# A transformer block on one core: a new order of TensorE's work in a step, a larger loop group, three moved operations and new places

## The chip, the cores and the metric

The kernel runs on one core of one Trainium2 chip. A core has TensorE (PE; its weight loads are PEld), VectorE (DVE), ScalarE (ACT), GpSimd (POOL) and SyncE (SP), which issues all the DMAs here. The metric is the device time of one execution in microseconds, the median of several. Everything is in fp32 but a few comparison results.

## The reference

For each of 32 images of 128 channels by 32 x 32 pixels (1024 tokens of 128 values), the reference computes:

```python
x = softmax(Q.T K / sqrt(C)) V + x               # full attention over the 1024 tokens
t = tokens(x)
n = layer_norm(t)
m = mamba(n, forward) + mamba(n reversed, backward)
t = t + m + leaky_relu(layer_norm(m) @ w1.T + b1) @ w2.T + b2
n = layer_norm(t)
w = n @ wr + br                                   # one weight per token
kept = the 511 tokens with the largest w
t = t + n + (w * (gelu(n @ f_w1 + b1) @ f_w2 + b2) where kept, else 0)
```

A mamba direction projects a token to 256 inner values, convolves 4 taps, applies silu, makes dt, B and C, and runs for each of 16 states a recurrence over the 1024 tokens, `h = exp(dt*A) * h + dt*B*u`, with `y = sum over states of C*h`. Then `y + x*D` is multiplied by `silu(z)` and projected back.

## The kernel before

**Tiling.** The mamba of an image is cut in four quarters k: two directions times two chunks of 512 tokens. Each quarter has 16 states, which gives 64 steps n an image. A step holds 256 inner values (two halves of 128 partitions) by 512 tokens for one state.

**A step on each engine.** ACT (`scale_u`, line 860) and POOL (`scale_u`, line 1042) make u*B for two blocks of tokens each, token-wise (`ub`). PE (`turn_ub`, line 518) turns it to channels in PSUM, one half after the other; half 0 waits for both makers, and each half waits until DVE's scan of the step before has read its bank. ACT (`decay`, line 848) makes exp(dt*A) of each half (`da`). DVE runs the recurrence as a scan of each half (`scan`, line 1160). POOL multiplies both halves by C (`times_c`, line 1056, result `g`), which SP has brought from DRAM by a DMA (`load_c`, line 461). PE turns g back and sums it over halves and states in PSUM (`add_y`, line 522), in two parts; part 0 waits for POOL's product, and the end of part 1 frees the buffer of g. ub, da, h and g have two buffers each. The u*B of step n+2 can be made when both halves of step n are turned.

**All the rest is laid between.** A step has four slots, so an image has slots 0 to 255. Tables at the top of the kernel (`AT_...`, `LN_...`) give each other operation its slot: the closing of a finished quarter (`AT_YT`, `AT_SKIP`, `AT_GATE`, `AT_M`), the preparation of the next (`AT_CONV` to `AT_UKEEP`), the attention of the next image (`AT_XT` to `AT_T1`), and the end of the image before (the layer norms, the first MLP, the token weights `AT_W`, their ranking `AT_RANK` and `AT_WK`, the mask `AT_WTIMES`, the second MLP `AT_HID` to `AT_FFN`, and the output). Every engine walks the slots in order, so a slot is a place in its queue, not a time. On PE `aside(SLOTS * n + i)` stands after the pieces of the step. `u_tok`, the token-wise u, is copied from PSUM by DVE at `AT_UKEEP` (line 1248), and the u*B of steps 16, 32, 48 and of the next image's first, made two steps earlier, waits for it. The mask: DVE counts for each token the heavier ones (lines 1275 to 1279), sums, compares with 511 (line 1286), and POOL multiplies the result with the weights (line 1108); DVE uses it in the last sum (line 1293).

**Groups.** `turns(first, count, ...)` emits `count` images in a row without a meeting of the engines. At its end the engines meet, and all semaphores are cleared. The first call has only the first image's attention and first quarter, the second is image 0, and a hardware loop runs groups of `JOINED` images over the next 30; then the last image and its end follow. Before all, one block loads the weights, and ACT and DVE fold some of them once all have landed.

The step on PE, lines 799 to 811:

```python
if n + 1 < ALL or nxt:
    turn_ub(n + 1, 0)
aside(SLOTS * n)
if n + 1 < ALL or nxt:
    turn_ub(n + 1, 1)
aside(SLOTS * n + 1)
if n or last:
    add_y(n - 1, 0)
aside(SLOTS * n + 2)
if n or last:
    add_y(n - 1, 1)
aside(SLOTS * n + 3)
```

Of the kernel before, what the change touches and what calls it, by code (L numbers as in the profile page):

```python
# [5 lines left out]
def conv_attn_mamba_mod_kernel(nc, I, out):  # L6
# [39 lines left out]
    JOINED = 5  # L46
# [4 lines left out]
    AT_YT = (4, 68, 132, 198)  # L51
    AT_SKIP = (8, 74, 137, 202)
    AT_GATE = ((6, 6), (84, 88), (136, 154), (203, 208))
    AT_CONV = ((8, 8, 8, 9), (75, 76, 79, 81), (135, 136, 137, 152), (204, 205, 205, 205))
    AT_PROJ = (17, 74, 140, 203)
    AT_PROJKEEP = (21, 80, 143, 203)
    AT_TAPS = ((25, 26, 27), (84, 87, 87), (148, 156, 158), (208, 209, 209))
    AT_XC = (24, 86, 156, 210)
    AT_Z = ((27, 27), (86, 86), (156, 157), (157, 157))
    AT_ZKEEP = (24, 86, 157, 157)  # L60
    AT_ROWS = ((28, 28), (88, 91), (158, 163), (211, 211))
    AT_ROWKEEP = (28, 95, 164, 213)
    AT_M = ((13, 13), (92, 95), (164, 164), (212, 212))
    AT_MKEEP = (19, 98, 168, 216)
    AT_B = (32, 97, 168, 215)
    AT_BKEEP = (37, 103, 172, 218)
    AT_DT = (35, 101, 170, 215)
    AT_DTCUT = (39, 106, 175, 219)
    AT_DTEXP = (38, 106, 174, 217)
    AT_DTLN = (38, 112, 177, 217)  # L70
    AT_DTMAX = (47, 117, 182, 223)
    AT_U = (51, 118, 183, 226)
    AT_DTKEEP = (51, 116, 180, 231)
    AT_UT = (49, 118, 183, 239)
    AT_UKEEP = (54, 122, 186, 242)
    AT_CSTORE = (22, 114, 171, 212)

    AT_XT = 3
    AT_XTOK = 13
    AT_Q = (11, 12)  # L80
    AT_QKEEP = 12
    AT_K = (19, 20)
    AT_KKEEP = 23
    AT_V = (24, 27)
    AT_VKEEP = 32
    AT_S = (36, 37, 48, 48, 60, 61, 81, 81, 109, 109, 118, 118, 132, 134, 154, 154)
    AT_MAX = (43, 52, 66, 87, 114, 122, 139, 163)
    AT_EXP = (39, 52, 65, 90, 113, 122, 139, 168)
    AT_PT = (43, 52, 67, 96, 114, 124, 144, 173)
    AT_PTKEEP = (42, 55, 67, 97, 115, 123, 145, 174)  # L90
    AT_RINV = (47, 55, 74, 110, 118, 133, 148, 178)
    AT_PV = (46, 47, 55, 56, 68, 70, 106, 107, 116, 116, 127, 131, 148, 148, 178, 179)
    AT_T1 = (50, 61, 83, 110, 120, 133, 153, 182)

    LN_STATS = {0: (131, 194), 1: (15, 30), 2: (211, 213)}
    LN_AGGR = {0: (154, 195), 1: (16, 44), 2: (212, 213)}
    LN_POW = {0: 192, 1: 48, 2: 211}
    LN_APPLY = {0: (197, 197), 1: (58, 67), 2: (216, 216)}
    LN_TURN = {0: 199, 1: 182, 2: 217}
    LN_KEEP = {0: 201, 1: 180, 2: 217}  # L100

    AT_MT = (24, 30)
    AT_B2 = (29, 68)
    AT_T1OLD = 38
    AT_W1 = (184, 185, 189, 189)
    AT_HID1 = (184, 190)
    AT_LEAKY = (191, 195)
    AT_W2 = (195, 195, 195, 195)
    AT_T2 = 199
    AT_BASE = (221, 222)  # L110
    AT_W = (222, 222)
    AT_WKEEP = 221
    AT_WTURN = 225
    AT_WCOL = 229
# [7 lines left out]
    AT_T3 = (243, 247)  # L122
    AT_OUT = 246
    AT_OUTKEEP = 248
    AT_STORE = 244
# [9 lines left out]
    FIRST_T1 = tuple(FIRST + 6 + 4 * i for i in range(8))  # L135

# [5 lines left out]
    with ctx:  # L142
# [127 lines left out]
        zeroed = ctx.enter_context(nc.semaphore("zeroed"))  # L270
        setup_exp = ctx.enter_context(nc.semaphore("setup_exp"))


        with nc.Block() as block:
            loads = [
                (wq[:], I["wq"]), (wk[:], I["wk"]), (wv[:], I["wv"]),
                (bq[:], I["bq"]), (bk[:], I["bk"]),
                (bv_rows[:], I["bv"].to_broadcast([P, C])),
# [20 lines left out]
            @block.sync  # L299
            def _(sp):  # L300
                with nc.allow_non_contiguous_dma(reason="weights, once"):
                    for dst, src in loads:
                        sp.dma_start(dst, src).then_inc(loaded, 16)
                sp.wait_ge(loaded, 16 * len(loads))
# [14 lines left out]
            @block.scalar  # L319
            def _(act):  # L320
                act.wait_ge(loaded, 16 * len(loads))
                act.activation(a_neg[:], a_neg[:], ACT.Exp).then_inc(setup_exp, 1)

            @block.vector
            def _(dve):
                dve.wait_ge(loaded, 16 * len(loads))

                dve.tensor_scalar(bq[:], bq[:], SCALE, None, ALU.mult)
                dve.tensor_scalar(b1_low[:], b1[:], SLOPE, None, ALU.mult)
                dve.tensor_copy(wr_cols[:], wr[:].to_broadcast([C, P]))  # L330

                for r in range(DIRS):
                    for tap in range(KCONV):
                        dve.tensor_tensor(w_conv[:, r, tap, :], w_conv[:, r, tap, :], in_cols[:, r, 0:P], ALU.mult)
                dve.wait_ge(setup_exp, 1)
                dve.tensor_scalar(a_neg[:], a_neg[:], -1.0, None, ALU.mult)
# [65 lines left out]
            (w_col_kept, 1), (w_kept_made, 1), (w_made, 1), (w_row_kept, 1), (w_turned, 1), (x_loaded, 16),  # L402
# [9 lines left out]
        def turns(first, count, last, now, nxt):  # L412
# [32 lines left out]
            with nc.Block() as block:  # L445

                def sp_turn(sp, j):
# [31 lines left out]
                    if nxt:  # L479
                        sp.dma_start(x_in[:], I["x"][image + 1]).then_inc(x_loaded, 16)  # L480
# [25 lines left out]
                def pe_turn(pe, j):  # L506
# [103 lines left out]
                    def prepare(at, k):  # L610
# [3 lines left out]
                        if at == AT_PROJ[k]:  # L614
                            if k == QUARTERS - 1:
# [6 lines left out]
                        for tap in due(AT_CONV[k], at):  # L622
                            if tap == 0 and k == QUARTERS - 1:
# [104 lines left out]
                    def attend_next(at):  # L728
                        if at == AT_XT:
                            pe.wait_ge(x_loaded, since(x_loaded, 16))  # L730
# [93 lines left out]
                def act_turn(act, j):  # L824
# [52 lines left out]
                    def prepare(at, k):  # L877
# [133 lines left out]
                    if not now:  # L1011
                        for at in range(SLOTS * ALL):
                            aside(at)
                        if nxt:
                            for n in range(LEAD):
# [9 lines left out]
                def pool_turn(pool, j):  # L1025
# [50 lines left out]
                    def aside(at):  # L1076
# [8 lines left out]
                        if last:  # L1085
# [52 lines left out]
                def dve_turn(dve, j):  # L1138
# [71 lines left out]
                    def prepare(at, k):  # L1210
# [35 lines left out]
                        if at == AT_UKEEP[k]:  # L1246
                            dve.wait_ge(u_turned, since(u_turned, prep(k, 1, 1)))
                            dve.tensor_copy(u_tok[:, side, :, :].rearrange("p b d -> p (b d)"), banks(Y)  # L1248
                                            ).then_inc(u_kept, 1)

                    def finish_last(at):
# [29 lines left out]
                        if at == AT_WK:  # L1281
# [4 lines left out]
                            dve.tensor_scalar(is_kept[:], rank[:], float(KEPT), None, ALU.is_lt).then_inc(ranked, 1)  # L1286
                        for part in due(AT_T3, at):
                            if part == 0:
                                dve.wait_ge(w_kept_made, since(w_kept_made, 1))
# [50 lines left out]
                    if not now:  # L1340
                        for at in range(SLOTS * ALL):
                            aside(at)
# [70 lines left out]
```

## Time and profile before

| what | us |
|---|---|
| median of 3 runs | 8347.58 (8346.27 to 8347.81) |
| the profiled execution | 8358.25 |
| its span | 8356.5 |
| from the span's start to the first scan | 135.0 |
| image 0, scan to scan | 240.8 |
| an image inside a group | 252.8 |
| the 32nd image's first scan to the end | 356.8 |

The page gives for each engine its busy time over the span; a view by stretches gives the same for any piece of it, with the clock granted to PE (1.00 is full speed), which shows which engine is full where. The view in order of time gives start and length of groups of instructions. Matmul rows are modelled to their ends and overlap, so the distance of their starts says more of PE's cost than their length. Places in the image are named by the first scan of its steps: image 18 begins at 4697.6, and its pieces of 8 steps begin at 4697.6, 4729.8, 4758.6, 4788.3, 4817.6, 4845.6, 4877.1 and 4911.6.

### The profile page before, as it was taken

What the parts mean: (1) busy time and instruction counts of PE and PEld (TensorE: products, weight loads), DVE (VectorE), ACT (ScalarE), POOL (GpSimd) and SP (SyncE); (2) the same over time, 40 slices, a digit from 0 to 9 for tenths busy, and PEclk for the clock granted to TensorE, in tenths of its full rate; (3) what the DMA queues carried; (4) which work ended last, traced back from release to release, by engine and by line L of the source; (5) the groups of instructions that cost most, each with busy time, mean ns of one, the idle gap of its engine ahead of it and who ended that gap; (6) DMA issues with size and microseconds to landing.
All of it is one profiled execution on the core that took longest, in us unless ns stands there. A gap on an engine that the chain in (4) does not pass through costs nothing. (4 is left out here: it accounts for less than half of the span.)

```text
span 8356.5 us, 152516 instructions
## 1 busy us (share of the span) xinstructions
PE 7891.8 (94%) x53760; PEld 6159.6 (74%) x53760; DVE 7365.4 (88%) x10156; ACT 6933.8 (83%) x11874; POOL 7487.6 (90%) x7051
## 2 busy tenths in 40 slices
PE   6999999999999999999999999999999999999986
PEld 4777777777777777777777777777777777777765
DVE  4899899898999898999989999989999989999985
ACT  4888888888888888888888888888888888888874
POOL 3999999899999899999999999989999999999985
PEclk9999999999999999999999999999999999999998
DMA  1222222222222222222222222222222222222221
GB/s 49 75 68 79 75 76 73 71 72 77 75 74 74 72 73 76 74 74 69 73 78 75 74 75 72 73 75 74 74 75 72 74 75 74 74 71 72 78 71 35
DMA packets 321339, 604.11 MB, mean 72 GB/s; under 512 B 40961, under 2 KB 43714, under 8 KB 320578
## 3 DMA queue, kind: packets, MB, share of 16 engines
q1 hardware_dynamic: 320578, 594.31, 23.0%
q8 instruction: 435, 7.13, 0.4%
q14 instruction: 326, 2.67, 0.1%
HBM read 556.42 MB, written 20.97 MB: 69 GB/s over the span
## 5 line engine op out<-in xcount | busy, mean ns | idle before, releaser
L1056 POOL TENSOR_TENSOR g<-h,c_all 128x1024 f32<-128x1024 f32 x2048 | 4861.9, 2374 | 210.4 <-DVE h L1160 119.6
L848 ACT ACTIVATE da<-dt,a_neg 128x512 f32<-128x512 f32 x4096 | 2771.4, 715 | 165.4 <-DVE h L1160 158.4
L1160 DVE TENSOR_TENSOR_SCAN h<-da,ps 128x512 f32<-128x512 f32 x2048 | 2432.2, 1210 | 447.2 <-ACT da L848 215.1
L1160 DVE TENSOR_TENSOR_SCAN h<-da,h,ps 128x512 f32<-128x512 f32 x2048 | 2544.8, 1270 | 214.7 <-PE ps L518 80.4
L518 PE MATMUL ps<-ident,ub 128*128 128x128 f32 x16384 | 2373.2, 276 | 126.0 <-DVE h L1160 107.0
L518 PEld LDWEIGHTS ps<-ident,ub 128*128 128x128 f32 x16384 | 1886.0, 141 | 761.7 <-issue 466.4
L522 PE MATMUL ps<-ident,g 128*128 128x128 f32 x16384 | 2248.7, 275 | 12.8 <-POOL g L1056 9.4
L522 PEld LDWEIGHTS ps<-ident,g 128*128 128x128 f32 x16384 | 1892.0, 141 | 421.3 <-issue 391.1
L1042 POOL TENSOR_SCALAR ub<-u_tok,b_tok 128x256 f32<-128x256 f32 x4096 | 1932.8, 488 | 208.9 <-DVE u_tok L1248 190.4
L860 ACT ACTIVATE ub<-u_tok,b_tok 128x256 f32<-128x256 f32 x4096 | 1845.8, 500 | 310.0 <-PE ps L518 219.5
L515 PE MATMUL ps<-v_tok,probs_t 128*128 128x128 f32 x4096 | 543.3, 278 | 16.4 <-ACT probs_t L966 16.4
L515 PEld LDWEIGHTS ps<-v_tok,probs_t 128*128 128x128 f32 x4096 | 491.5, 192 | 34.5 <-ACT probs_t L966 30.4
L515 PE MATMUL ps<-k_all,q 128*128 128x512 f32 x1024 | 502.1, 598 | 7.5 <-DVE t L1315 3.1
L515 PE MATMUL ps<-x_pad,w_conv 128*128 128x512 f32 x1024 | 504.9, 595 | 0.2 <-DVE xc L1193 0.2
L837 ACT ACT_TABLE_LOAD x352 | 451.6, 1283 | 6.2
L972 ACT ACTIVATE probs<-ps,nmax 128x1024 f32<-128x1024 f32 x256 | 284.5, 1111 | 106.8 <-DVE nmax L1303 100.8
L1303 DVE TENSOR_REDUCE nmax<-ps 128x1 f32<-128x1024 f32 x256 | 308.7, 1206 | 40.5 <-PE ps L515 40.5
L966 ACT ACTIVATE probs_t<-ps 128x1024 f32<-128x1024 f32 x256 | 262.2, 1024 | 86.5 <-PE ps L518 84.3
L1083 POOL TENSOR_TENSOR xc<-xc,sz 128x512 f32<-128x512 f32 x256 | 326.4, 1281 | 6.2 <-DVE xc L1193 6.2
L518 PE MATMUL ps<-ident,probs 128*128 128x128 f32 x2048 | 270.7, 275 | 59.5 <-ACT probs L972 59.5
L515 PE MATMUL ps<-tile_b,f_w 128*128 128x512 f32 x512 | 261.0, 633 | 63.4 <-ACT hid L945 40.1
L1218 DVE SCALAR_TENSOR_TENSOR ps<-x_proj,w_taps,ps 128x512 f32<-128x512 f32 x384 | 283.8, 739 | 25.8 <-ACT ps L890 12.4
(125 smaller groups left out, 9152.8 us busy)
## 6 DMA issues: line engine op xcount, KB each, us to landing
c_all<-c_rows SPq DMA_DIRECT2D x2048, 256.0 KB, 3.1
x_in<-in_x SPq DMA_DIRECT2D x32, 512.0 KB, 5.6
t_old<-t SPq DMA_DIRECT2D x32, 512.0 KB, 4.4
out<-tile_b SPq DMA_DIRECT2D x32, 512.0 KB, 2.8
c_rows<-rows SPq DMA_DIRECT2D x128, 32.0 KB, 2.7
w_conv<-in_conv_rows SPq DMA_DIRECT2D x1, 512.0 KB
f_w<-in_f_w SPq DMA_DIRECT2D x2, 256.0 KB
hid<-in_in_proj SPq DMA_DIRECT2D x1, 256.0 KB
```

The costliest lines, as they stand in the source:

```text
L515: return nc.tensor.matmul(o, a, b, start=first, stop=last)
L518: return nc.tensor.transpose(o, src, ident[:])
L522: return nc.tensor.matmul(o, src, ident[:], start=first, stop=last, is_transpose=True)
L837: nc.scalar.preload_act_table_set(name)
L848: act.activation(da[:, n % 2, half, :], dt[:, slot, half, :], ACT.Exp, scale=a_neg[:, r, half, s:s + 1]).then_inc(da_made, 1)
L860: t = act.activation(ub[:, n % 2, b, :], u_tok[:, slot, b, :], ACT.Copy, scale=b_tok[:, slot, b, s:s + 1])
L972: act.activation(probs[:], banks(att(i)), ACT.Exp, bias=nmax[:, i:i + 1], accum_out=rowsum[:, i:i + 1]).then_inc(probs_made, 1)
L1042: t = pool.tensor_scalar(ub[:, n % 2, b, :], u_tok[:, slot, b, :], b_tok[:, slot, b, s:s + 1], 1.0, ALU.mult, ALU.mult)
L1056: pool.tensor_tensor(g[:, n % 2, :, :], h[:, n % 2, :, at:at + BANK], c_all[:, n % RING, :].unsqueeze(1).to_broadcast([P, NH, BANK]), ALU.mult
L1083: pool.tensor_tensor(xc[:, slot, half, :], xc[:, slot, half, :], sz[:, slot % NCH, half, :], ALU.mult).then_inc(y_gated, 1)
L1160: dve.tensor_tensor_scan(h[:, n % 2, half, at:at + BANK], da[:, n % 2, half, :], ps[:, DB + half, :], before, ALU.mult, ALU.add).then_inc( ...
L1303: dve.tensor_reduce(nmax[:, i:i + 1], banks(att(i)), AX.X, ALU.max, negate=True).then_inc(max_made, 1)
```

## The change

Five things change.

- On PE, the sum's part 1 (`add_y(n - 1, 0)`) moves between the halves of u*B: a step is now half 0, sum part 1, half 1, sum part 2, with a slot after each.
- `JOINED` is 15 for 5.
- The first block waits on DVE for seven loads alone (x of image 0, now first, and the attention's weights); x of image 0 is no longer loaded in the first turn. The folding of the other weights moves to the first turn, at slot 60 on ACT and DVE, and PE's first quarter and ACT's first u*B wait for it (`weights_made`).
- The copy of u_tok goes from DVE to ACT; the mask's product goes from POOL to DVE, as eight products of one column.
- Nearly all places are new.

```diff
-    JOINED = 5
+    JOINED = 15
...
-    AT_CONV = ((8, 8, 8, 9), (75, 76, 79, 81), (135, 136, 137, 152), (204, 205, 205, 205))
+    AT_CONV = ((7, 7, 7, 8), (78, 81, 81, 83), (140, 141, 142, 152), (209, 210, 210, 210))
-    AT_GATE = ((6, 6), (84, 88), (136, 154), (203, 208))
+    AT_GATE = ((7, 7), (80, 87), (160, 160), (209, 213))
-    AT_Z = ((27, 27), (86, 86), (156, 157), (157, 157))
+    AT_Z = ((24, 25), (85, 85), (160, 160), (160, 161))
-    AT_DTCUT = (39, 106, 175, 219)
+    AT_DTCUT = (42, 103, 174, 225)
-    AT_DTMAX = (47, 117, 182, 223)
+    AT_DTMAX = (47, 112, 178, 230)
-    AT_UT = (49, 118, 183, 239)
+    AT_UT = (53, 117, 180, 236)
-    AT_UKEEP = (54, 122, 186, 242)
+    AT_UKEEP = (54, 116, 180, 236)
-    AT_B2 = (29, 68)
+    AT_B2 = (27, 97)
-    AT_BASE = (221, 222)
+    AT_BASE = (225, 227)
-    AT_EARLIER = 223
+    AT_EARLIER = 229
-    AT_RANK = (230, 231, 231, 232, 234, 234, 234, 239)
+    AT_RANK = (235, 235, 237, 238, 238, 238, 239, 240)
-    AT_WK = 240
-    AT_WTIMES = 237
+    AT_WK = 243
-    AT_HID = (226, 226, 229, 229, 231, 231, 232, 232)
-    AT_GELU = (227, 227, 228, 228)
-    AT_FFN = (233, 233, 233, 234, 239, 239, 240, 242)
+    AT_HID = (230, 230, 232, 232, 235, 235, 236, 236)
+    AT_GELU = (231, 233, 233, 233)
+    AT_FFN = (239, 239, 239, 239, 241, 241, 242, 242)
...
+            first_loads = [
+                (x_in[:], I["x"][0]), (bq[:], I["bq"]), (wq[:], I["wq"]), (bv_rows[:], I["bv"].to_broadcast([P, C])),
+                (wk[:], I["wk"]), (bk[:], I["bk"]), (wv[:], I["wv"]),
+            ]
...
+                dve.wait_ge(first_loaded, 16 * len(first_loads))
...
                         aside(SLOTS * n)
+                        if n or last:
+                            add_y(n - 1, 0)
+                        aside(SLOTS * n + 1)
                         if n + 1 < ALL or nxt:
                             turn_ub(n + 1, 1)
-                        aside(SLOTS * n + 1)
-                        if n or last:
-                            add_y(n - 1, 0)
                         aside(SLOTS * n + 2)
...
+                        if at == AT_UKEEP[k]:
+                            act.wait_ge(u_turned, since(u_turned, prep(k, 1, 1)))
+                            act.activation(u_tok[:, side, :, :].rearrange("p b d -> p (b d)"), banks(Y), ACT.Copy
+                                           ).then_inc(u_kept, 1)
...
+                            if nxt and at == SETUP:
+                                act.wait_ge(loaded, all_loaded)
+                                tables("natural_log_exp_and_others")
+                                act.activation(a_neg[:], a_neg[:], ACT.Exp).then_inc(setup_exp, 1)
...
-                            if at == AT_WTIMES:
-                                pool.wait_ge(ranked, since(ranked, 1))
-                                pool.tensor_tensor(w_kept[:], is_kept[:], w_col[:], ALU.mult).then_inc(w_kept_made, 1)
...
+                            dve.wait_ge(ranked, since(ranked, 1))
+                            for i in range(NB):
+                                dve.tensor_scalar(w_kept[:, i:i + 1], is_kept[:, i:i + 1], w_col[:, i:i + 1], None, ALU.mult
+                                                  ).then_inc(w_kept_made, 1)
```

## Rows read from the trace of the kernel before

**Rows 1.** Busy time of each engine over the span, with instructions, from the page.

```profile
PE 7891.8 (94%) x53760; PEld 6159.6 (74%) x53760; DVE 7365.4 (88%) x10156; ACT 6933.8 (83%) x11874; POOL 7487.6 (90%) x7051
```

**Rows 2.** Busy time, clock and DMA by stretch: image 18, three of eight pieces.

```profile
4697.60:4729.80 32.20, 31.43 (x202) 23.30 (x200) 26.37 (x36) 24.48 (x41) 32.20 (x31) 1.00 0.24 81
4877.10:4911.60 34.50, 33.95 (x231) 26.34 (x232) 32.70 (x55) 32.55 (x61) 33.83 (x37) 1.00 0.20 63
4911.60:4950.40 38.80, 35.40 (x234) 26.80 (x233) 36.97 (x75) 28.79 (x46) 28.94 (x27) 1.00 0.22 64
```

**Rows 3.** In order of time, image 18, steps 15 to 17 (start us, length us).

```profile
4757.62 1.02 PE L515 MATMUL ps<-k_all,q 128*128 128x512 f32 x2
...
4758.48 0.60 PE L518 MATMUL ps<-ident,ub 128*128 128x128 f32 x4
...
4758.92 1.02 PE L515 MATMUL ps<-k_all,q 128*128 128x512 f32 x2
...
4759.24 2.37 POOL L1056 TENSOR_TENSOR g<-h,c_all 128x1024 f32<-128x1024 f32 x1
...
4760.65 1.09 PE L518 MATMUL ps<-ident,ub 128*128 128x128 f32 x8
...
4764.37 2.44 DVE L1160 TENSOR_TENSOR_SCAN h<-da,h,ps 128x512 f32<-128x512 f32 x2
```

**Rows 4.** The same view, behind a boundary of the loop's groups.

```profile
1648.63 0.90 PE L518 MATMUL ps<-ident,ub 128*128 128x128 f32 x3 [4.17 <-DVE h L1160]
```

**Rows 5.** By stretch: last and first image at a boundary, then a plain one.

```profile
1390.50:1647.40 256.90, 245.37 (x1692) 192.04 (x1689) 229.92 (x318) 217.12 (x373) 234.80 (x223) 1.00 0.24 74
1647.40:1902.20 254.80, 245.82 (x1670) 193.87 (x1671) 230.00 (x317) 215.87 (x371) 232.92 (x219) 0.98 0.23 73
4697.60:4950.40 252.80, 244.30 (x1682) 191.09 (x1681) 229.91 (x317) 216.36 (x372) 233.90 (x221) 1.00 0.24 74
```

**Rows 6.** By stretch: the first 5.35 us behind that boundary.

```profile
1647.35:1652.70 5.35, 4.07 (x18) 3.68 (x19) 3.65 (x4) 4.88 (x8) 5.35 (x4) 0.50 0.66 204
```

**Rows 7.** In order of time: the start of the kernel.

```profile
17.78 1.96 SPq L303 DMA_DIRECT2D w_rows<-in_x_proj  x3
...
21.65 0.15 DVE L328 TENSOR_SCALAR bq<-bq 128x1 f32<-128x1 f32 x1 [21.65 <-DMA w_rows<-in_x_proj]
...
27.61 1.97 PE L518 MATMUL ps<-ident,x_in 128*128 128x128 f32 x8 [27.61 <-DMA x_in<-in_x]
```

**Rows 8.** Who waited for whom: us in total, times, longest us.

```profile
POOL w_kept L1108 <- DVE is_kept L1286: 249.0, 32, 13.4
...
PEld ps L518 <- DVE h L1160: 208.2, 401, 4.6
POOL ub L1042 <- DVE u_tok L1248: 190.4, 64, 28.5
```

**Rows 9.** Groups of instructions by line: busy us, mean ns | idle before, releasers.

```profile
L1056 POOL TENSOR_TENSOR g<-h,c_all 128x1024 f32<-128x1024 f32 x2048 | 4861.9, 2374 | 210.4 <-DVE h L1160 119.6 <-PE ps L522 67.4 <-issue 17.9
...
L1042 POOL TENSOR_SCALAR ub<-u_tok,b_tok 128x256 f32<-128x256 f32 x4096 | 1932.8, 488 | 208.9 <-DVE u_tok L1248 190.4 <-PE ps L518 15.1 <-POOLq L1350 3.5
...
L1277 DVE TENSOR_SCALAR_CACHE_REDUCE compared<-w_row,w_col 128x1024 bf16<-128x1024 f32 (+7 forms) x256 | 207.4, 810 | 0.5 <-POOL tile_a L1103 0.5
...
L1238 DVE SCALAR_TENSOR_TENSOR ps<-ps,b_dt,dt 128x512 f32<-128x512 f32 x256 | 179.2, 746 | 3.9 <-ACT dt L915 2.2
...
L1275 DVE TENSOR_SCALAR_CACHE_REDUCE compared<-w_row,w_col 128x128 bf16<-128x128 f32 (+6 forms) x224 | 164.7, 735 | 0.0
...
L1248 DVE COPY u_tok<-ps 128x1024 f32<-128x1024 f32 x128 | 154.5, 1207 | 3.8 <-PE ps L518 3.7
...
L919 ACT ACTIVATE dt<-ps 128x1024 f32<-128x1024 f32 x128 | 130.3, 1018 | 58.7 <-DVE u L1245 58.7
...
L1279 DVE TENSOR_SCALAR_CACHE_REDUCE tied<-tile_a,w_col 128x128 bf16<-128x128 f32 x256 | 88.1, 344 | 0.0
...
L1279 DVE DVE_READ_ACCUMULATOR tied<-tile_a,w_col 128x1 f32 x256 | 21.8, 85 | 0.0
```

More of the change, by code:

```diff
@@ L74, in conv_attn_mamba_mod_kernel @@
-    AT_UT = (49, 118, 183, 239)
-    AT_UKEEP = (54, 122, 186, 242)
-    AT_CSTORE = (22, 114, 171, 212)
-    AT_XT = 3
[L79 to L102, printed above, removed]
@@ L122, in conv_attn_mamba_mod_kernel @@
[L122 to L125, printed above, removed]
+    AT_YT = (4, 68, 132, 197)
+    AT_SKIP = (7, 74, 140, 202)
+    AT_GATE = ((7, 7), (80, 87), (160, 160), (209, 213))
+    AT_CONV = ((7, 7, 7, 8), (78, 81, 81, 83), (140, 141, 142, 152), (209, 210, 210, 210))
+    AT_PROJ = (14, 74, 144, 209)
+    AT_PROJKEEP = (18, 81, 150, 210)
+    AT_TAPS = ((20, 24, 24), (82, 82, 86), (154, 160, 161), (212, 215, 215))
+    AT_XC = (23, 83, 159, 214)
+    AT_Z = ((24, 25), (85, 85), (160, 160), (160, 161))
@@ new lines, in conv_attn_mamba_mod_kernel @@
+    AT_ZKEEP = (24, 85, 159, 160)
+    AT_ROWS = ((28, 31), (88, 89), (162, 165), (215, 216))
+    AT_ROWKEEP = (33, 88, 165, 217)
+    AT_M = ((10, 10), (90, 91), (166, 166), (217, 217))
+    AT_MKEEP = (15, 97, 171, 220)
+    AT_B = (36, 97, 169, 220)
+    AT_BKEEP = (40, 100, 173, 223)
+    AT_DT = (39, 99, 170, 220)
+    AT_DTCUT = (42, 103, 174, 225)
+    AT_DTEXP = (41, 101, 174, 223)
+    AT_DTLN = (41, 101, 174, 225)
+    AT_DTMAX = (47, 112, 178, 230)
+    AT_U = (50, 114, 179, 230)
+    AT_DTKEEP = (52, 114, 177, 232)
@@ new lines, in conv_attn_mamba_mod_kernel @@
+    AT_UT = (53, 117, 180, 236)
+    AT_UKEEP = (54, 116, 180, 236)
+    AT_CSTORE = (43, 90, 157, 205)
+    AT_XT = 3
+    AT_XTOK = 8
+    AT_Q = (16, 18)
+    AT_QKEEP = 20
+    AT_K = (21, 23)
+    AT_KKEEP = 24
+    AT_V = (28, 28)
+    AT_VKEEP = 29
+    AT_S = (33, 34, 44, 44, 62, 62, 77, 83, 106, 106, 120, 122, 136, 138, 158, 158)
+    AT_MAX = (39, 48, 66, 87, 111, 126, 142, 164)
+    AT_EXP = (37, 49, 66, 90, 110, 124, 142, 172)
+    AT_PT = (39, 50, 67, 92, 110, 127, 148, 175)
+    AT_PTKEEP = (39, 53, 69, 99, 111, 127, 150, 174)
@@ new lines, in conv_attn_mamba_mod_kernel @@
+    AT_RINV = (44, 55, 74, 101, 120, 130, 158, 183)
+    AT_PV = (42, 42, 55, 58, 71, 73, 100, 103, 113, 115, 131, 131, 154, 155, 176, 178)
+    AT_T1 = (46, 63, 77, 107, 121, 137, 158, 184)
+    LN_STATS = {0: (130, 190), 1: (12, 17), 2: (208, 210)}
+    LN_AGGR = {0: (160, 190), 1: (14, 42), 2: (208, 214)}
+    LN_POW = {0: 197, 1: 44, 2: 215}
+    LN_APPLY = {0: (198, 201), 1: (62, 77), 2: (218, 218)}
+    LN_TURN = {0: 206, 1: 184, 2: 224}
+    LN_KEEP = {0: 207, 1: 184, 2: 224}
+    AT_MT = (18, 40)
@@ new lines, in conv_attn_mamba_mod_kernel @@
+    AT_B2 = (27, 97)
+    AT_T1OLD = 28
+    AT_W1 = (188, 190, 195, 195)
+    AT_HID1 = (190, 194)
+    AT_LEAKY = (195, 199)
+    AT_W2 = (199, 199, 199, 203)
+    AT_T2 = 207
+    AT_BASE = (225, 227)
+    AT_W = (227, 227)
+    AT_WKEEP = 226
+    AT_WTURN = 230
+    AT_WCOL = 233
+    AT_EARLIER = 229
[4 more added lines that the diff above has]
+    AT_FFN = (239, 239, 239, 239, 241, 241, 242, 242)
@@ L128, in conv_attn_mamba_mod_kernel @@
+    AT_T3 = (245, 246)
+    AT_OUT = 247
+    AT_OUTKEEP = 249
+    AT_STORE = 240
     FIRST = SLOTS * 12
@@ L135, in conv_attn_mamba_mod_kernel @@
     FIRST_T1 = tuple(FIRST + 6 + 4 * i for i in range(8))
+    SETUP = FIRST + 12
     def due(slots, g):
@@ L270, in conv_attn_mamba_mod_kernel @@
         zeroed = ctx.enter_context(nc.semaphore("zeroed"))
+        first_loaded = ctx.enter_context(nc.semaphore("first_loaded"))
         setup_exp = ctx.enter_context(nc.semaphore("setup_exp"))
+        weights_made = ctx.enter_context(nc.semaphore("weights_made"))
         with nc.Block() as block:
+            first_loads = [
+                (x_in[:], I["x"][0]), (bq[:], I["bq"]), (wq[:], I["wq"]), (bv_rows[:], I["bv"].to_broadcast([P, C])),
+                (wk[:], I["wk"]), (bk[:], I["bk"]), (wv[:], I["wv"]),
+            ]
             loads = [
-                (wq[:], I["wq"]), (wk[:], I["wk"]), (wv[:], I["wv"]),
-                (bq[:], I["bq"]), (bk[:], I["bk"]),
-                (bv_rows[:], I["bv"].to_broadcast([P, C])),
                 (in_cols, I["in_proj"][:, :, 0:DI].rearrange("r c e -> c r e")),
@@ L301, in _ @@
                 with nc.allow_non_contiguous_dma(reason="weights, once"):
+                    for dst, src in first_loads:
+                        sp.dma_start(dst, src).then_inc(first_loaded, 16)
                     for dst, src in loads:
                         sp.dma_start(dst, src).then_inc(loaded, 16)
-                sp.wait_ge(loaded, 16 * len(loads))
             @block.gpsimd
@@ L316, in _ @@
                                    base=0, pattern=[[-1, P]], channel_multiplier=1)
[L319 to L322, printed above, removed]
             @block.vector
             def _(dve):
-                dve.wait_ge(loaded, 16 * len(loads))
+                dve.wait_ge(first_loaded, 16 * len(first_loads))
                 dve.tensor_scalar(bq[:], bq[:], SCALE, None, ALU.mult)
[L329 to L336, printed above, removed]
+        all_loaded = 16 * len(loads)
         x_loaded, stored = sem("x_loaded"), sem("stored")
@@ L401, in conv_attn_mamba_mod_kernel @@
             (u_made, 4), (u_turned, 4), (ub_made, 64), (ub_made_pool, 64), (v_kept, 1), (v_made, 1),
-            (w_col_kept, 1), (w_kept_made, 1), (w_made, 1), (w_row_kept, 1), (w_turned, 1), (x_loaded, 16),
+            (w_col_kept, 1), (w_kept_made, 8), (w_made, 1), (w_row_kept, 1), (w_turned, 1), (x_loaded, 16),
             (xc_kept, 8), (xc_made, 4), (xt_kept, 1), (xt_made, 1), (y_gated, 8), (y_kept, 4), (y_made, 64),
@@ L478, in sp_turn @@
                         sp.wait_ge(v_made, since(v_made, 0))
-                    if nxt:
+                    if nxt and now:
                         sp.dma_start(x_in[:], I["x"][image + 1]).then_inc(x_loaded, 16)
@@ L614, in prepare @@
                         if at == AT_PROJ[k]:
+                            if not now:
+                                pe.wait_ge(weights_made, 1)
                             if k == QUARTERS - 1:
@@ L622, in prepare @@
                         for tap in due(AT_CONV[k], at):
+                            if tap == 0 and not now:
+                                pe.wait_ge(weights_made, 1)
                             if tap == 0 and k == QUARTERS - 1:
@@ L729, in attend_next @@
                         if at == AT_XT:
-                            pe.wait_ge(x_loaded, since(x_loaded, 16))
+                            if now:
+                                pe.wait_ge(x_loaded, since(x_loaded, 16))
                             if joined:
@@ L1012, in act_turn @@
                         for at in range(SLOTS * ALL):
+                            if nxt and at == SETUP:
+                                act.wait_ge(loaded, all_loaded)
+                                tables("natural_log_exp_and_others")
+                                act.activation(a_neg[:], a_neg[:], ACT.Exp).then_inc(setup_exp, 1)
                             aside(at)
                         if nxt:
+                            act.wait_ge(weights_made, 1)
                             for n in range(LEAD):
@@ L1245, in prepare @@
                             dve.tensor_tensor(u[:], ps[:, Y:Y + NH, :], xc[:, slot, :, :], ALU.mult).then_inc(u_made, 1)
[L1246 to L1249, printed above, removed]
                     def finish_last(at):
@@ L1286, in finish_last @@
                             dve.tensor_scalar(is_kept[:], rank[:], float(KEPT), None, ALU.is_lt).then_inc(ranked, 1)
+                            dve.wait_ge(ranked, since(ranked, 1))
+                            for i in range(NB):
+                                dve.tensor_scalar(w_kept[:, i:i + 1], is_kept[:, i:i + 1], w_col[:, i:i + 1], None, ALU.mult
+                                                  ).then_inc(w_kept_made, 1)
                         for part in due(AT_T3, at):
                             if part == 0:
-                                dve.wait_ge(w_kept_made, since(w_kept_made, 1))
+                                dve.wait_ge(w_kept_made, since(w_kept_made, NB))
                             dve.wait_ge(base_made, since(base_made, part + 1))
@@ L1341, in dve_turn @@
                         for at in range(SLOTS * ALL):
+                            if nxt and at == SETUP:
+                                dve.wait_ge(loaded, all_loaded)
+                                dve.tensor_scalar(b1_low[:], b1[:], SLOPE, None, ALU.mult)
+                                dve.tensor_copy(wr_cols[:], wr[:].to_broadcast([C, P]))
+                                for r in range(DIRS):
+                                    for tap in range(KCONV):
+                                        dve.tensor_tensor(w_conv[:, r, tap, :], w_conv[:, r, tap, :], in_cols[:, r, 0:P],
+                                                          ALU.mult)
+                                dve.wait_ge(setup_exp, 1)
+                                dve.tensor_scalar(a_neg[:], a_neg[:], -1.0, None, ALU.mult).then_inc(weights_made, 1)
                             aside(at)
```

28 lines of the change are left out of this document (removed).

## The prediction

> **What bounds the kernel now.** I read the page's busy shares first. PE is busy 94% of the span, POOL 90%, DVE 88%, ACT 83% [rows 1]: no engine has room by itself, so the question is which one is full in which stretch. An image inside a group of the loop takes 252.8 us, from its first scan to the next image's first scan. The view by stretches cuts one such image in pieces of 8 steps. In the first piece POOL is busy 32.20 of 32.20 us, in the seventh 33.83 of 34.50, and in the eighth DVE 36.97 of 38.80 while POOL works 28.94 [rows 2]. So POOL sets the pace early, POOL and PE together in the middle, DVE at the end. In the first and the seventh piece PE too is 98% busy by the view, but a matmul's row there carries its latency: the two of 512 columns at 4757.62 show 1.02 us and the flips behind them start 0.86 later; four flips of u*B show 0.60 and what follows starts 0.44 later [rows 3].
>
> Were the view's PE row a floor (244.3 of 252.8, the sum of all eight pieces), nothing could win over 8.5 us an image. The Trainium skill, "Perfetto Trace Analysis", section Identifying the Most-Contended Engine, says that matmul busy time is no measure of PE's headroom and that the share of weight loading is. Weight loading is 74% here [rows 1], so by that rule the ceiling is the busier of POOL and DVE. My forecast stays below both ceilings.
>
> **Part 1, the loop's group.** JOINED goes from 5 to 15, so 30 images take 2 groups for 6 and four boundaries go. At one, PE stands 4.17 us for the first scan behind it [rows 4]. The image that ends at it takes 256.9 us and the one after it 254.8, beside 252.8 for a plain one [rows 5]: 4.1 + 2.0. The second loss need not recur in full, so I take 5.2 us (bounds 4.1 and 6.1): 4 x 5.2 = 21 us (16 to 24). Part of the 2.0 is the clock: over the 5.35 us after the stop, PE's granted clock is 0.50, the 1.2 GHz level [rows 6]; it is 1.00 in the pieces of a plain image [rows 2].
>
> **Part 2, the start.** The first block now waits for nothing but issues the same 33 loads and one for x. Those end at 17.78 + 1.96 = 19.7 us [rows 7], plus some 0.45 for x; DVE waits for seven of them. If the block still ends in a meeting of all engines, PE's first flip moves from 27.61 to about 20.5: 7.1 us less. The weight set-up on DVE and ACT, 2.1 us from 21.65 [rows 7] on by its eleven short operations, moves into the first attention. That chain is serial, and DVE waits in it, so between none and all of the 2.1 returns. I take 6 us (5 to 7). If engines could leave the block alone, x, issued first, would set the start and up to 19 us would go; I don't count on it.
>
> **Part 3, work that changes engine, per image.** Four copies of u_tok leave DVE (1.207 us each by mean, -4.8) and come to ACT, whose nearest row, the copy of dt from the same PSUM banks, takes 1.018 us: +4.1 on ACT. w_kept leaves POOL: its wait for is_kept was 249.0 us in 32, 7.8 an image [rows 8], and DVE gets eight one-column products and a wait. Nearest rows: one-column reads at 85 ns [rows 9] and the 344 ns of the 128-column comparison; by the 85 they are 0.7 us, and I take 1.1 with the wait, bounds 0.7 and 2.8. DVE's balance is -3.7. POOL's 7.8 us of waiting is in the eighth piece, where DVE is full, so its loss is cover: it is worth nothing by itself, and what is late next is the ranking on DVE. POOL's waits for u_tok are 190.4 us; less the 28.5 of the start they are 5.2 an image [rows 8]. The copies moved from slots 122, 186, 242 to 116, 180, 236, ahead of the u*B that needs them at 120, 184, 248, so most of that wait goes; what follows on POOL there is the same products, and DVE is as full in those steps. ACT's own queue behind each copy is the decay of two steps later.
>
> **Part 4, the places.** I laid every instruction of both tables into its step, with its row's time (POOL: 2.374 for g, 2 x 0.47 for u*B, and for a half sum or a gate, with half of g's columns, 1.28; DVE: 1.2 a scan, 1.4 for a pair of 746 ns operations, 16.5 for the ranking, from 207.4 + 164.7 + 88.1 over 32 and 23 or 24 reads of 85 ns; PE: 0.44 for four flips, 0.86 for 512 columns, and for four products a tenth more than that) [rows 3, 9], scaled each engine to its busy time of the image, and took the largest engine in each 8 steps. Before: 32.3 POOL, 28.3 POOL, 29.8 POOL, 27.8 DVE, 30.6 PE, 27.0 PE, 36.8 POOL, 39.0 DVE = 251.7 us; the trace has 252.8, and 32.2, 34.5 and 38.8 in the pieces shown [rows 2]. After: 31.0, 29.6, 29.9, 27.3, 27.3, 29.4, 33.2, 41.6 = 249.2 us. The first loses half of the bias sum (slot 68 to 97). The fifth hands four gate products (3.4 us of PE) to the sixth. The seventh loses three POOL operations (two half sums and the mask of earlier weights) to the eighth, where POOL has room. The eighth gains on DVE, the bound there: the cut and the maximum of dt go from slots 219 and 223 to 225 and 230, +2.8, less the u_tok copy, plus the products. The same count in stretches of 4 steps gives -1.3 and of 16 steps -1.8. I take -2.0 us an image (-0.5 to -3.5).
>
> **Part 5, PE's order.** Sum part 1 now stands between the halves of u*B. Two edges. For it: PE waits for DVE's scan 208.2 us in 401 times [rows 8], of which seven boundaries are some 30; going through image 18 in order of time, 4 of its 5 us are ahead of half 1, and a sum can fill them. Against it: the sum needs POOL's product, and half 1 comes 0.44 us later, with what the slot holds. In one step of the image the product ends at 4761.61 and half 1 started at about 4761.09: the sum would wait 0.5 us; but the scan's pair that eats this half started its first part at 4764.37 and so had over 2 us [rows 3]. In 13 of its 64 steps the product is late by the new order, 5.7 us in all, mostly in such slack. SP, ACT and POOL keep their order. I take 0, with -4 and +4.5 us an image as bounds.
>
> **Sum.** 30 full images and the last: 31 x 2.0 = 62; 62 + 21 + 6 = 89. The profiled execution took 8358.25 us with a span of 8356.5, so it would come to 8269; the median of the runs is 10.7 below it, 8347.58, and gives 8259, say 8260 us.
>
> **Rivals.** (a) Only the loop and the start pay, and the places balance better on paper than on queues with waits: 8348 - 27 = 8321. For it: DVE, bound at the end, gets longer there. 18%. (b) The sums fill PE's waits as well, 4 us an image more: 8259 - 124 = 8135. For it: the 4 us; against it, POOL and DVE are full while PE waits. 12%. (c) Slower than before: sum part 1 holds half 1. Price: 13 late products and a later half 1 in the 19 steps of this image where its scan followed within 0.5 us (19 x 0.44 = 8.4); half of the 14.1 together, less the half of PE's own 5 us of waits that goes, is 4.5 us an image, and 2.5 after the 2.0 of the places. Then 8348 - 27 + 31 x 2.5 = 8398. It decides from 2.9 us an image (89 / 31) onward. Against it: where POOL is full, its u*B is what PE would wait for next anyway. 12%. (d) The clock. The ranks stood at slots 230 to 239 and now at 235 to 240, four of them (8.3 us) between two scans, where PE has 5.6 us of work (four flips, four of the sum, half the second MLP's output with 0.9 for its bias) before it needs the next scan. PE would stand for 8.3 + 1.2 - 5.6 = 3.9 us, as at a boundary, and a clock of 0.50 for 5.35 us [rows 6] costs 2.7 us of PE an image: 8259 + 31 x 2.7 = 8343. 8%, since PE, 35.40 of 38.80 us busy in this piece [rows 2], may come late to that place. The Trainium skill, "TensorE: Matmul & The Clock Gate", section Part 1: The HAM clock gate, says the same of idling: the lower level is the default and activity lifts it; the trace agrees at the boundary.
>
> **How the numbers follow.** Forecast 8260 at 50%; its own range, by the bounds of parts 1 to 4, is 8205 to 8310. The range for 8 in 10 is 8160 to 8345: it takes in (a) and (d), leaves out (c) and most of (b). About 0.2% (17 us) is what a measurement of this kernel tells from no change. Faster by more: 50 + 18 + 12 = 80%; within: (d), 8%; slower: 12%.
>
> **What would show it.** Right: one boundary inside the loop and a plain image of about 250.8 us; PE's first flip near 20.5 us; POOL with no wait for is_kept and hardly one for u_tok; the last 8 steps longer by 1 to 3 us, the seventh piece shorter. Wrong: PE waiting for POOL's product over 3 us an image, DVE's scans waiting for PE more than before, or a granted clock below 1.00 near step 60.

## The result

| | us, median of the runs compared |
|---|---|
| before | 8346.37 |
| after | 8371.96 |
| ratio | 1.0031, 95% interval 1.0023 to 1.004 |
| predicted | 8260 (8160 to 8345) |

The kernel is 25.6 us slower, where 89 us less were forecast. The profiled execution of after has a span of 8379.3 us. Against [rows 1], its page has 100 us more on ACT and 33 less on DVE, and PE and POOL are as busy as before.

```profile
PE 7892.6 (94%) x53760; PEld 6152.6 (73%) x53760; DVE 7332.3 (88%) x10284; ACT 7034.2 (84%) x12002; POOL 7481.8 (89%) x7019
```

The view by stretches, in its columns as in [rows 2]: first the whole of image 20 of after, then its third, sixth, seventh and eighth pieces of 8 steps (the third begins at step 16), and the image that ends at the one boundary left in the loop.

```profile
5216.70:5470.90 254.20, 244.34 (x1681) 191.03 (x1682) 228.86 (x321) 219.58 (x376) 233.61 (x220) 1.00 0.24 74
...
5277.60:5309.50 31.90, 31.53 (x205) 23.71 (x206) 26.86 (x27) 28.53 (x54) 30.54 (x29) 1.00 0.25 74
5363.30:5395.50 32.20, 31.29 (x216) 24.06 (x215) 27.41 (x41) 28.94 (x48) 28.45 (x26) 1.00 0.23 67
5395.50:5428.70 33.20, 32.06 (x215) 24.38 (x214) 30.11 (x45) 30.63 (x57) 32.54 (x34) 1.00 0.20 62
5428.70:5470.90 42.20, 38.52 (x252) 28.59 (x250) 41.22 (x86) 32.49 (x50) 29.53 (x28) 1.00 0.17 55
...
3935.40:4194.60 259.20, 245.87 (x1692) 192.42 (x1692) 228.91 (x322) 220.31 (x377) 234.56 (x222) 1.00 0.24 74
```

An image grew where [rows 5] has 252.8: this one takes 254.2, and 254.7 is the median of images 2 to 30, boundaries included. The last 8 steps take 42.2 us for 38.8 and DVE is busy in 41.22 of them [rows 2]. The seventh piece fell by 1.3 us to the 33.2 forecast, where the count had let it fall by 3.6, from 36.8; the third, forecast at 29.9, takes 31.9, and the sixth, forecast at 29.4, takes 32.2.

The view in order of time around the mask shows what fills DVE's last piece.

```profile
5458.08 2.35 POOL L1064 TENSOR_TENSOR g<-h,c_all 128x1024 f32<-128x1024 f32 x1 [5.45 <-DVE h L1165]
5458.11 2.37 DVE L1287 TENSOR_SCALAR is_kept<-rank 128x8 f32<-128x8 f32 x1
...
5460.51 1.06 DVE L1290 TENSOR_SCALAR w_kept<-is_kept,w_col 128x1 f32<-128x1 f32 x8
```

Eight numbers a partition take 2.37 us, from 0.03 us behind the start of POOL's product to 0.05 behind its end. All 32 executions of this comparison, in the view of its tile, in before and in after:

```profile
L1286 DVE TENSOR_SCALAR is_kept<-rank x32: 171/172/174, 617.1 to 8335.7; 128x8 f32<-128x8 f32 x32
...
L1287 DVE TENSOR_SCALAR is_kept<-rank x32: 172/2362/2369, 611.8 to 8355.8; 128x8 f32<-128x8 f32 x32
```

The columns are least, median and most in ns. In after 31 of the 32 last 2355 or more, and each of them starts 0.02 to 0.03 us behind a product of POOL; the one of the last image, with nothing on POOL beside it, lasts 172 as all did before. It never shows as a wait, since the profile counts it as busy.

Last, who waited for whom in after. DVE's scans wait 341.7 us for PE where they waited 181 in before, and PE waits 281.5 us (its weight loads) for POOL's product, 8.8 an image.

```profile
POOL g L1064 <- DVE h L1165: 403.0, 339, 5.5
DVE h L1165 <- PE ps L512: 341.7, 559, 2.3
PEld ps L516 <- POOL g L1064: 281.5, 490, 4.1
ACT ub L859 <- PE ps L512: 277.4, 330, 4.1
...
POOL ub L1050 <- ACT u_tok L921: 30.7, 2, 29.8
```

### The profile page after: what moved, and what is told of

It is laid out like the page before. It is cut to its first block and busy times, and to the rows that moved or that the text cites. A ratio compares the mean times of both kernels' runs of the same rounds, so it can differ in the third digit from the quotient of the medians.

```text
span 8379.3 us, 152633 instructions
## 1 busy us (share of the span) xinstructions
PE 7892.6 (94%) x53760; PEld 6152.6 (73%) x53760; DVE 7332.3 (88%) x10284; ACT 7034.2 (84%) x12002; POOL 7481.8 (89%) x7019
## 5 line engine op out<-in xcount | busy, mean ns | idle before, releaser
L516 PE MATMUL ps<-ident,g 128*128 128x128 f32 x16384 | 2496.5, 275 | 148.4 <-POOL g L1064 144.4
L512 PE MATMUL ps<-ident,ub 128*128 128x128 f32 x16384 | 2489.1, 275 | 77.3 <-DVE h L1165 64.1
L516 PEld LDWEIGHTS ps<-ident,g 128*128 128x128 f32 x16384 | 1919.3, 141 | 809.2 <-issue 519.7
L512 PEld LDWEIGHTS ps<-ident,ub 128*128 128x128 f32 x16384 | 1915.6, 141 | 510.6 <-issue 409.3
L1050 POOL TENSOR_SCALAR ub<-u_tok,b_tok 128x256 f32<-128x256 f32 x4096 | 1912.0, 480 | 180.2 <-PE ps L512 144.2
L509 PE MATMUL ps<-v_tok,probs_t 128*128 128x128 f32 x4096 | 539.4, 278 | 36.8 <-ACT probs_t L969 36.8
```

Of the source, the lines that this page charges most:

```text
L509: return nc.tensor.matmul(o, a, b, start=first, stop=last)
L512: return nc.tensor.transpose(o, src, ident[:])
L516: return nc.tensor.matmul(o, src, ident[:], start=first, stop=last, is_transpose=True)
L1050: t = pool.tensor_scalar(ub[:, n % 2, b, :], u_tok[:, slot, b, :], b_tok[:, slot, b, s:s + 1], 1.0, ALU.mult, ALU.mult)
```

## The experiments

Times are medians; the change against before is taken against the runs of before on the same chip (8347.92, 8350.27, 8348.48 and 8353.36 us in the four groups below). Where two runs are compared, each is first taken against its own before. The interval of a ratio is some 0.1% to either side, 8 to 13 us. The diffs show the main lines, without all conditions and increments of semaphores; `...` stands for lines left out.

### First group: the mask, the order, the loop

**a_mask_fused**, on the kernel after:

```diff
-dve.tensor_scalar(is_kept[:], rank[:], float(KEPT), None, ALU.is_lt).then_inc(ranked, 1)
-dve.wait_ge(ranked, since(ranked, 1))
 for i in range(NB):
-    dve.tensor_scalar(w_kept[:, i:i + 1], is_kept[:, i:i + 1], w_col[:, i:i + 1], None, ALU.mult)
+    dve.tensor_scalar(w_kept[:, i:i + 1], rank[:, i:i + 1], float(KEPT), w_col[:, i:i + 1], ALU.is_lt, ALU.mult)
```

> The kernel after, with is_kept left out: the eight one-column products of the mask compare the rank and multiply by the weight in one instruction each. In the trace of after, is_kept lasts 2.36 us (0.17 before) and ends with POOL's product of g. Theory M (the mask): DVE's comparison of SBUF to SBUF cannot run beside POOL's product and costs DVE, which is full there, 2.2 us an image; without it 31 x 2.2 = 68 us go: 8372 - 68 = 8304. Theory O (the order of PE) and theory P (the places): DVE's time there is covered by others, under 15 us go: 8357 to 8372.

Measured: 8336.48 us, ratio to before 0.9986 (0.9977 to 0.9995). Against after, each on its own before, 37 us are gone. That is half of the 68: the comparison blocked DVE for 31 x 2.2 us, and half of what was freed doesn't show in the time: the median of images 2 to 30 falls by 1.1 us, from 254.7 to 253.6. The last piece of image 20 shows 40.70 us for 42.20, with DVE no longer full:

```profile
5407.00:5447.70 40.70, 37.82 (x252) 28.69 (x250) 39.11 (x86) 31.85 (x49) 29.63 (x28) 1.00 0.17 55
```

**a_order_old**, on the kernel after (and **b_order_new** its reverse, on the kernel before):

```diff
+turn_ub(n + 1, 1)
+aside(SLOTS * n + 1)
 add_y(n - 1, 0)
-aside(SLOTS * n + 1)
-turn_ub(n + 1, 1)
```

> The kernel after with PE's old order in a step (both halves of u*B, then both sum parts); all else as in after. Theory O: the sum's wait for POOL (426 us in the rows of after against 36 before) and the later half 1 (DVE's scans wait 342 us for PE against 181) cost 1 to 2 us an image; the old order gives 30 to 60 us back: 8312 to 8342. Theory M and theory P: the order is a wash or the new places need it, 8360 to 8400.

Measured: 8471.63 us, 1.0148 (1.0132 to 1.0164). The new places need the new order: 98 us more than after, and above both ranges.

> The kernel before with the new order of PE alone, its own places kept. Theory O: slower by 1 to 3 us an image, 8380 to 8440. The prediction's bounds were -4 to +4.5 us an image. Theory M: within 20 us of before, 8326 to 8366.

Measured: 8903.83 us, 1.0664 (1.0649 to 1.0679), 556 us more, 18 an image, four times the bound that the prediction gave the order and far above both ranges. Its waits:

```profile
DVE h L1160 <- PE ps L518: 711.4, 919, 4.0
ACT ub L860 <- PE ps L518: 699.0, 623, 3.8
...
POOL ub L1042 <- PE ps L518: 402.2, 353, 6.9
```

In before these are 181, 219 and 15 us.

**b_joined**, on the kernel before, `JOINED = 15`.

> The kernel before with groups of 15 images for 5. The prediction: four boundaries at 5.2 us go, 21 us (16 to 24): 8325. Rival, since images inside the groups of after vary less but one of them (17) took 258.0 us: what a boundary costs comes back elsewhere, 8340 to 8350.

Measured: 8323.11 us, 0.9970 (0.9958 to 0.9981). 24.8 us for four boundaries, 6.2 each, near the whole 4.1 + 2.0 of [rows 5] (16 to 35 us in all, by the interval). It didn't come back elsewhere, as the rival had it.

### Second group: the ring of u*B, and the outer part alone

**b_order_new_ub4** and **a_fused_ub4**, with `UBS = 4`:

```diff
-ub = sb("ub", [P, 2, QB, DI])
+ub = sb("ub", [P, UBS, QB, DI])
... # PE, ACT and POOL take buffer n % UBS for n % 2
-if now and (n > LEAD or joined):
-    act.wait_ge(dbx_made, since(dbx_made, NH * (n - 2)))
+if now and (n > UBS or joined):
+    act.wait_ge(dbx_made, since(dbx_made, NH * (n - UBS)))
```

> The kernel before with the new order of PE, and four buffers for u*B in place of two; the makers of u*B still run two steps ahead. In the new order alone (8904 us) ACT waits 699 us and POOL 402 us for PE before u*B, beside 219 and 15. Theory R (the ring): half 1 is turned later, that frees the buffer of u*B later, and ACT and POOL, which make the next u*B in their queues' order, stop with all that stands behind it. With four buffers that wait is gone, and most of the 557 us: 8340 to 8500. Theory H (half 1): the scans of half 1 get their data later, whatever the buffers: 8750 to 8900.

Measured: 8743.98 us, 1.0469 (1.0453 to 1.0485). 162 of the 556 us go, 394 stay: between the two ranges, 6 us below the second. Both theories hold a part.

> The kernel after with the mask of one instruction a column (8336 us) and four buffers for u*B. There ACT waits 320 and POOL 144 us for PE before u*B. Theory R: part of these 464 us is on the path even with the new places, 1 to 3 us an image: 8245 to 8305. Theory P (the places were made for two buffers, and the stops are covered by others): 8320 to 8340.

Measured: 8336.71 us, 0.9987 (0.9978 to 0.9997), the same as with two buffers. With the places made for the order, the ring isn't on the path.

**b_outer**: the kernel before with `JOINED = 15`, the seven first loads, and the folding in the first turn; order, places, u_tok and the mask as in before.

> The kernel before with groups of 15 images and the start of after (first loads, folding in the first turn); order, places, u_tok's copy and the mask as before. Groups alone gave 8323; the first scan comes at 131.8 us in after for 135.0. So 8323 - 3 = 8320 by that, 8317 by the 6 us of the prediction.

Measured: 8316.40 us, 0.9962 (0.9949 to 0.9976). **b_outer_fused** puts the mask on it in a_mask_fused's form, at slot 240, and takes POOL's wait away:

> The same with the mask on DVE, one instruction a column (eight, some 0.12 us each). POOL's wait for the comparison, 7.8 us an image, goes, and DVE, full there, gets 1 us an image. The prediction's reading (the wait is cover, DVE is the bound): 8320 + 31 x 1 = 8351. Rival: POOL's stop holds the products and then the scans (DVE waits for POOL's g 101 us in before), so that up to 2 us an image come back: 8290 to 8325.

Measured: 8320.40 us, 0.9966 (0.9952 to 0.9980), not to be told from b_outer. The 31 us that the prediction's reading gave DVE's products don't appear. Either POOL's 7.8 us of waiting an image were cover and the products cost little, or a small gain and a small cost cancel; this run can't tell the two apart. The blocked comparison isn't in it.

### Third group: which part of the order costs, and where u_tok is copied

**b_sum_only** and **b_slot_only**, on the kernel before:

```diff
 turn_ub(n + 1, 0)
 aside(SLOTS * n)
+add_y(n - 1, 0)            # b_sum_only
+aside(SLOTS * n + 1)       # b_slot_only
 turn_ub(n + 1, 1)
-aside(SLOTS * n + 1)       # b_slot_only
-add_y(n - 1, 0)            # b_sum_only
```

> The kernel before with sum part 1 between the halves of u*B, and the work of slot 1 behind half 1, as before: half 1 comes 0.44 us later and waits for POOL's product, and nothing else comes between. The full new order cost 557 us. Theory S (the slot's work): the 29 us of an image's PE work that stand in slots 1 now hold half 1, and the scans of half 1; the sum alone costs under 150: 8350 to 8500. Theory W (the sum and its wait for the product): 8650 to 8900.

Measured: 8460.57 us, 1.0131 (1.0116 to 1.0147), 112 us more.

> The kernel before with the work of slot 1 ahead of half 1 and the sum where it was. Theory S: most of the 557 us: 8600 to 8850. Theory W: under 8500.

Measured: 8734.29 us, 1.0464 (1.0448 to 1.0480), 386 us more. 112 + 386 = 498 of 556: two thirds of the order's price on old places are the work of slot 1 that now precedes half 1, a fifth is the sum with its wait, and the rest is what they do together. In b_sum_only the scans' waits for PE are 316 us in 615 times; the sum is cheap, but not free.

**b_outer_uact**: b_outer with `AT_UKEEP = (54, 119, 183, 242)`, the copy on ACT as in after. **a_fused_udve**: a_mask_fused with the copy back on DVE, at the slots of after.

> The kernel before with groups of 15 and the new start (8316 us) and u_tok's copy on ACT, at slots 54, 119, 183 and 242 (119 and 183 for 122 and 186, since ACT needs its own copy at 120 and 184). The prediction: DVE loses 4.8 us an image and POOL's 5.2 us of waiting for u_tok go. Where DVE is full at these places, 1 to 2 us an image: 8254 to 8285. Rival: the copy needs the flips of u at slots 118 and 183, so ACT stops for PE and with it the decays behind: 8300 to 8340.

Measured: 8354.60 us, 1.0009 (1.0000 to 1.0018), 40 us more than b_outer, and above both ranges.

> The kernel after with the mask of one instruction a column (8336 us) and u_tok's copy back on DVE, same slots. If the move to ACT was worth the 4.8 us of DVE where DVE is full: 31 x 1 to 2 = 8367 to 8398. If the move brought nothing: 8325 to 8345.

Measured: 8742.20 us, 1.0472 (1.0458 to 1.0486), 405 us more than a_mask_fused, and far above both ranges. Either move costs time: neither table bears the other's engine. The waits say in part why. The first row is b_outer_uact, where POOL's wait for u_tok stays at the 190 us and more of before, since the slots hardly moved (and DVE's scans wait 260.8 us for PE, for 177.0 in b_outer):

```profile
POOL ub L1051 <- ACT u_tok L922: 211.9, 65, 29.8
```

and this one is a_fused_udve, where DVE reaches the copy before PE has made the flips, and stops with its scans behind it:

```profile
DVE u_tok L1249 <- PE ps L512: 312.9, 128, 4.5
```

### Fourth group: the new places, the form of the comparison, the ring in the old order

**a_fused_slot_behind**: a_mask_fused with `add_y(n - 1, 0)`, `turn_ub(n + 1, 1)`, then `aside(SLOTS * n + 1)` and `aside(SLOTS * n + 2)`.

> The kernel after with the mask of one instruction a column (8336 us), and the work of slot 1 behind half 1 in place of ahead of it, as in b_sum_only. On the places of before, the slot's work ahead of half 1 cost 386 us and the sum 112. If it costs in the kernel after too (DVE's scans wait there 343 us for PE), the time falls below the 8316 us of the old order and old places: 8230 to 8310. If the new places keep light steps' work in slot 1 and count on it, the swap brings nothing or costs: 8330 to 8420.

Measured: 8417.18 us, 1.0075 (1.0062 to 1.0088), 75 us more than a_mask_fused, each on its own before. Giving half 1 its data earlier costs time with these places.

**a_mask_cols**: after, with is_kept in eight comparisons of one column.

> The kernel after, with is_kept made as eight comparisons of one column in place of one of eight columns; the eight products stay. Theory of the blocked comparison: it is the form with eight columns that can't run beside POOL's product, so eight short ones, seven instructions more and 0.7 us more of DVE an image, still come out near the kernel with no is_kept at all (8336): 8335 to 8355. If DVE's stop were one for the count or the wait on its own result, not for the form, it stays or grows: 8370 to 8395.

Measured: 8342.06 us, 0.9986 (0.9977 to 0.9995), the ratio of a_mask_fused. The same place in image 20, in order of time: eight comparisons in 0.58 us, beside POOL's product of 2.36.

```profile
5434.17 2.36 POOL L1064 TENSOR_TENSOR g<-h,c_all 128x1024 f32<-128x1024 f32 x1 [5.45 <-DVE h L1165]
...
5434.19 0.58 DVE L1288 TENSOR_SCALAR is_kept<-rank 128x1 f32<-128x1 f32 x8
...
5434.80 1.06 DVE L1292 TENSOR_SCALAR w_kept<-is_kept,w_col 128x1 f32<-128x1 f32 x8
```

It is the form that was blocked, not the count of instructions. The Trainium skill, "SBUF — State Buffer", section Who interferes with whom, says that DVE and GpSimd share a second pair of SBUF ports, that a `tensor_scalar` can run in a mode which takes it, and that the second to issue stands until the first is done. Both traces agree with the blocking: 2.36 us with eight columns; with one column, 0.14 us each and no stop. In which mode an instruction ran, no trace here shows.

**b_outer_ub4**: b_outer with four buffers of u*B.

> The kernel before with groups of 15, the new start (8316 us) and four buffers for u*B. In before ACT waits 219 us for PE ahead of u*B, 6.5 an image. In the new order alone four buffers gave 160 us back, in the kernel after none. If part of the 219 is on the path of the old order: 8270 to 8305. If ACT's stops are covered: 8310 to 8322.

Measured: 8315.08 us, 0.9953 (0.9941 to 0.9966), b_outer again, within the intervals. The two are the fastest versions of the study, 34 to 38 us under before, with the order and the places of before.

## Why the prediction was wrong

By differences to before, the result closes. The loop and the start give 33.9 us (b_outer), the order, the places, u_tok's copy and the mask's move together cost 22.4 (from there to a_mask_fused, at -11.4), and the blocked comparison costs 37.0 (from there to after, at +25.6). The forecast had -27, -62 and nothing for the three. So the miss, 114 us, is made of 84 by the places and the order (parts 3 to 5) and 37 by the comparison, less the 7 that the outer part gave beyond its forecast.

**Part 1, right, a little low.** 24.8 us for 21, just above the upper bound of 24 and within the noise of it.

**Part 2, right in its mechanism.** The first block still ends in a meeting; PE's first flip comes at 21.25 us for 20.5 forecast and 27.61 before.

```profile
18.60 1.96 SPq L310 DMA_DIRECT2D w_rows<-in_x_proj  x3
...
21.25 1.94 PE L512 MATMUL ps<-ident,x_in 128*128 128x128 f32 x8 [21.25 <-PEq L277]
```

The first scan moved by 3.2 us in after and 5.3 in b_outer (129.7 for 135.0); in a_mask_fused, with the start of after, it moved by 5.8, so one execution gives it only within some us. b_outer is 7 to 9 us under b_joined's gain alone, for 6.

**Part 3, wrong in one price, and that turned a small gain into a loss.** "Nearest rows: one-column reads at 85 ns" priced the eight products, and rightly: 1.06 us as they stand. The comparison ahead of them got no price of its own; it had taken 0.17 us in before. Those executions had a quiet POOL: it stood waiting for that very instruction, 249.0 us in all [rows 8]. The step that failed is "its loss is cover: it is worth nothing by itself". For time b_outer_fused has nothing against it, but the wait also kept POOL off while DVE compared. In after, POOL's product starts with the end of the same scan that lets DVE go on, so the two meet in 31 of 32 images. The cost, 2.2 us an image in DVE's full piece, appears on the path with about half its size. POOL's waits for u_tok went as forecast, to 0.9 us beside the start's 29.8.

**Part 4, the step with the wrong sign, and the largest part of the miss.** "I took the largest engine in each 8 steps" gave 249.2 us an image, 2.5 less than its 251.7 for before. Without the blocked comparison the median of images 2 to 30 is 253.6 us, and 252.7 in b_outer: 0.9 more.

The count's gain stood mainly in the seventh piece (3.6 us) and the fifth (3.3). Just there it had laid too much on before: 36.8 and 30.6, where the trace has 34.5 and 28.0. Most of the gain was this excess; from b_outer to a_mask_fused the two pieces of image 20 give 1.2 and 1.4 us. The sixth was short in both, 27.0 for 31.5 before and 29.4 for 32.2 after. The third, with a change of 0.1 by the count, grew by 2.0 us: PE has more matmuls there and is busy nearly throughout. First b_outer, then a_mask_fused:

```profile
5238.00:5267.70 29.70, 29.03 (x188) 21.54 (x187) 26.44 (x26) 25.33 (x45) 29.70 (x28) 1.00 0.23 72
...
5255.90:5287.70 31.80, 31.43 (x205) 23.61 (x205) 26.82 (x26) 28.37 (x54) 30.46 (x29) 1.00 0.25 74
```

That the sum fitted before within 1.1 us was luck, misses of both signs, and I took the fit as a proof. Such a count knows how much work stands in 8 steps, not whether each piece is there when its reader comes, and it isn't even a floor for a piece, as the seventh and the fifth of before show. It gives the same 249.2 us for after and for after in the old order, which lie 98 us apart, and for a_mask_fused and a_fused_slot_behind, 75 apart. For a_fused_udve's 405 us it has at most the 4.8 us an image of the copies, 149.

**Part 5, the order, mis-sized by four on the places it was worked out from.** "Half 1 comes 0.44 us later, with what the slot holds" names the cause, and the sum then priced 0.44 us alone. The slot's work was the larger part (386 us of 556 on old places). And "SP, ACT and POOL keep their order. I take 0" left out who waits for half 1 beside the scan: both makers of u*B, for their buffer, with decays, exponentials and products queued behind (162 us by four buffers). The fill of PE's waits did occur, but at another's cost: in after PE's weight loads wait 65 us for DVE's scan, for 208, and 281 for POOL's product. On the new places nothing shows the order to be bad by itself; taking it back costs 98 us. Each table is made for its order and its engine, and swapping the order, a part of it or the copy's engine alone costs 40 to 556 us. What of the 22 us comes from the order, from the places and from u_tok's copy isn't settled: no run has good places for another mixture.

**Rivals.** (c), slower by the order, had the right sign and the signs in the waits, but its mechanism isn't shown as the cause: the old order on these places is slower still. The waits named as signs don't decide it either, since a_mask_fused, which is faster than before, has them too (343.4 us of the scans for PE, 300.3 of PE's weight loads for POOL). (d), the clock: PE didn't stand at the ranks. The granted clock of the last piece is 1.00; the second MLP's products fill the time between the two scans. (a) was right for the loop and the start (34 us for 27), but the places and the order, at nothing by it, cost 22, and it has no blocked comparison.

## What to carry to other kernels

Price an instruction that changes its neighbours by whom it will run beside, not by its old duration: a wait that costs nothing can be what keeps two instructions apart. A count of work per stretch can't rank two schedules that differ by less than its misses by piece; check those, not the sum, and look whether the gain stands where the count was wrong. For a reorder, list all who wait for the piece that is moved back, with everything that now stands ahead of it.

## What the runs showed of the hardware

- A DVE `tensor_scalar` of 128x8 fp32, SBUF to SBUF, takes 172 ns alone and 2.36 us beside a POOL multiplication of 128x1024 that started 0.02 to 0.03 us earlier (31 of 31); with 128x1 it takes 142 to 155 ns, beside the same multiplication or alone. The loss shows as busy time.
- A boundary of a loop of 5 or 15 images, with a meeting of all engines, costs 6.2 us (24.8 for four, 16 to 35 by the interval). By [rows 5] 4.1 us stand in the image that ends there and 2.0 in the next, where PE's granted clock is 0.50 (1.2 GHz) for the first 5.35 us [rows 6].
